# Finer scatter gates and earlier edge rows in the output stage of a graph network kernel

## What is computed

```python
h = jnp.maximum(_layernorm(x, axis=-1), 0.0)
...
h = _bn(jax.nn.relu(_gcn_conv(xn, src, dst, edge_weight, W1, b1, n)), g1, be1)
h = _bn(jax.nn.relu(_graph_conv(h, src, dst, edge_weight, Wrel2, brel2, Wroot2, n)), g2, be2)
h = _bn(jax.nn.relu(_graph_conv(h, src, dst, edge_weight, Wrel3, brel3, Wroot3, n)), g3, be3)
...
x = x + h
```

## Time and profile before

| | us |
|---|---|
| median of 3 runs | 3491.68 |
| the profiled execution, its own time | 3478.71 |
| its span, first to last instruction | 3476.9 |
| busy: TensorE, VectorE, ScalarE, GpSimd | 2853.6, 2650.0, 2361.0, 1376.2 |
| setup ends and `norm` starts at about | 38 |
| `norm` ends and `l1` starts at about | 483.6 |
| `out` starts at about | 2982 |

### The profile page before, as it was taken

One profiled execution on the slowest core, in us unless ns is written; L12 is line 12 of the kernel. 1 busy time (PEld: TensorE's weight loads), 2 busy tenths in 40 slices (PEclk: granted clock), 3 DMA queues, 4 the chain that ended last, 5 costly groups with the idle time before them and its releaser, 6 DMA issues. The chain is left out here.

```text
span 3476.9 us, 52252 instructions
## 1 busy us (share of the span) xinstructions
PE 2853.6 (82%) x12499; PEld 2035.4 (59%) x12641; DVE 2650.0 (76%) x5699; ACT 2361.0 (68%) x4168; POOL 1376.2 (40%) x1196
## 2 busy tenths in 40 slices
PE   3466549999999789999999999979999999544543
PEld 2455535555555467777777777656666666433432
DVE  6566638889898878888888888878999999533332
ACT  4577737777777578888888888667887887333331
POOL 1534556556666232111211111044433431266576
PEclk9788769999999899999999999999999999655555
DMA  5677638999999679999999999779999999799997
GB/s 195 219 244 267 228 129 315 356 329 360 343 360 355 254 283 350 351 358 352 364 355 356 355 355 357 254 269 329 353 355 358 358 351 334 285 366 361 381 357 231
DMA packets 335139, 1106.82 MB, mean 318 GB/s; under 512 B 54569, under 2 KB 102210, under 8 KB 285906
## 3 DMA queue, kind: packets, MB, share of 16 engines
q1 hardware_dynamic: 213412, 909.25, 71.3%
q0 software_dynamic: 62656, 77.70, 9.5%
q10 hardware_dynamic: 58990, 118.98, 9.4%
HBM read 599.13 MB, written 498.21 MB: 316 GB/s over the span
## 5 line engine op out<-in xcount | busy, mean ns | idle before, releaser
L1294 POOL DMA_INDIRECT l_ed_gathered<-agg_rows,pos_cols x392 | 457.4, 1167 | 1301.3 <-PE l_ps L1306 675.3
L1173 DVE TENSOR_TENSOR dense_tiles<-dense_tiles,l_dn_top 128x512 fp32r<-128x512 f32 x784 | 494.0, 683 | 140.6 <-ACT l_dn_top L1141 137.6
L1114 PE MATMUL l_ps<-l_dn_top,wroot_top 128*128 128x512 f32 x1176 | 485.6, 413 | 33.4 <-DVE dense_tiles L1173 14.0
L1114 PE MATMUL l_ps<-l_dn_top,wroot_rest 128*128 128x512 f32 x1176 | 467.6, 398 | 0.0
L1114 PE MATMUL l_ps<-dense_tiles,wroot_top 128*128 128x512 f32 x1176 | 466.8, 397 | 0.0
L1141 ACT ACTIVATE l_dn_top<-dense_tiles 128x512 fp32r<-128x512 f32 x784 | 447.7, 623 | 21.6 <-PEq L93 21.5
L640 PE MATMUL norm_ln_ps<-norm_ln_ho 128*128 128x130 f32 x1568 | 248.0, 321 | 183.1 <-ACT norm_ln_ho L628 100.3
L754 PE MATMUL l_ps<-l_dn_columns,w_fold 128*128 128x512 f32 x784 | 384.1, 612 | 9.9 <-ACT l_dn_ho L791 7.4
L628 ACT ACTIVATE norm_ln_ho<-norm_ln_x,norm_ln_nbias,norm_ln_rstd 128x128 f32<-128x128 f32 x784 | 304.0, 480 | 109.0 <-DVE norm_ln_nbias L581 105.9
L1763 PE MATMUL out_ps<-ident,dense_tiles 128*128 128x128 f32 x784 | 186.5, 417 | 205.7 <-ACT dense_tiles L1750 202.0
L1128 ACT ACTIVATE l_dn_ho<-l_ps,bias_fold 128x512 f32<-128x512 f32 x392 | 267.2, 685 | 128.5 <-PE l_ps L1114 124.5
(11 more groups left out here) (256 smaller groups left out, 6311.3 us busy)
## 6 DMA issues: line engine op xcount, KB each, us to landing
h_dense<-l_dn_ho SPq DMA_DIRECT2D x188, 1024.0 KB
dense_tiles<-h_dense SPq DMA_DIRECT2D x188, 1024.0 KB, 8.5
l_dn_rows<-h_rows SPq DMA_DIRECT2D x98, 520.0 KB
h_rows<-norm_ln_ho SPq DMA_DIRECT2D x97, 520.0 KB
h_dst<-l_ed_ho SPq DMA_DIRECT2D x98, 512.0 KB, 10.4
norm_ln_x<-in_x SPq DMA_DIRECT2D x97, 512.0 KB
x_tiles<-in_x SPq DMA_DIRECT2D x97, 512.0 KB, 6.4
out<-out_od_ot SPq DMA_DIRECT2D x97, 512.0 KB
```

Source lines behind the costliest of these rows:

```text
L1114: ins = pe.matmul(o, a, b, start=t == 0, stop=t == len(terms) - 1)
L1173: dve.tensor_tensor(rest[:, j, k, cc], hi[:, j, k, cc], top[:, j % 2, k, cc].bitcast(FP), ALU.subtract).then_inc(spl[j], 1)
L1294: pool.indirect_dma_start(tg[:, j, g, :], None, tab[n - 1][:, :], bass.IndirectOffsetOnAxis(ap=pos_c[:, t:t + 1], axis=0)).then_inc(gat[j] ...
```

## The change

Three things are changed.

First, in `out` the dense stages get a `head` of 4 slots, one round: the rows of edge chunks are made four tiles ahead. In the rounds of the order above the dense tiles stand one round later than before, and the edge chunks' scratch buffer lies in the memory of the statistics, which is free by then.

Second, in `norm` and in `out` the gate stands ahead of every chunk, and its unit is a **pair** of tiles (2048 nodes). The table has a row for each pair of slots.

Third, setup makes the table by integer shifts: last node, shifted right by 11, is the pair; shares of 2 or 4 slot pairs come by adding and shifting again.

```diff
+PAIR = 2 * W
-                sp.dma_start(last_node[:, 0:EI - 1], dst[0:(EI - 1) * ES * CW].rearrange("(o g e) -> o g e", o=1, g=EI - 1)[:, :, ES * CW - 1],
+                sp.dma_start(last_node[:, 0:EC - 1], dst[0:(EC - 1) * CW].rearrange("(o g e) -> o g e", o=1, g=EC - 1)[:, :, CW - 1],
...
-                for n in range(1, DI):
-                    dve.tensor_scalar(above[:, :, n - 1], last_f[:, :], float(n * NS * W), None, ALU.is_ge).then_inc(compared, 1)
-                dve.wait_ge(compared, DI - 1)
-                link(dve.tensor_reduce(count[:, 0, :], above[:, :, :], AXIS.X, ALU.add))
...
+                link(dve.tensor_scalar(last_pair[:, :], last_node[:, :], PAIR.bit_length() - 1, None, ALU.logical_shift_right))
+                for n in range(2):
+                    dve.tensor_scalar(shares_first[:, n, :], last_pair[:, :], 1, 2 - n, ALU.mult, ALU.add).then_inc(compared, 1)
...
-            firsts = [pool.value_load(table[0:1, row, g:g + 1], min_val=0, max_val=most) for row, (most, _) in enumerate(parts)]
-            for first, (_, slots) in zip(firsts, parts):
+            counts = [pool.value_load(table[0:1, row, g:g + 1], min_val=1, max_val=most) for row, (most, _) in enumerate(parts)]
+            for count, (_, slots) in zip(counts, parts):
                 for s in slots:
-                    pool.wait_ge(s, first * per + per)
+                    pool.wait_ge(s, count * per)
...
-                        if t % (ES * EG) == 0:
-                            gated(pool, rounds_norm, t // (ES * EG), 16, ((LI - 1, stored[0:2]), (LI - 2, stored[2:4]), (LI - 2, stored[4:8])))
+                        if t % EG == 0:
+                            gated(pool, tiles_norm, t // EG, 16, ((LI, stored[0:2]), (LI - 1, stored[2:4]), (LI - 1, stored[4:6]), (LI - 1, stored[6:8])))
...
+            head = slots if dense else 0
...
-                return slots, [(0, load)] + ([(slots - 1, store)] if dense else []), end if dense else None
+                return slots, [(head, load)] + ([(head + slots - 1, store)] if dense else []), end if dense else None
...
                     for k in range(EC):
                         pool.wait_ge(sm[k % slots], k // slots + 1)
-                        if k % ES == 0:
-                            gated(pool, rounds_first, k // ES, 16, ((DI - 1, dense_stored[0:2]), (DI - 2, dense_stored[2:4])))
+                        gated(pool, tiles_first, k, 16, ((DI, dense_stored[0:2]), (DI - 1, dense_stored[2:4])))
...
-                return slots, [(0, affine)], None
+                return slots, [(head, affine)], None
```

More of the change, by code:

```diff
@@ L279, in build @@
         ew_c = sb("weight_cols", [P, ET])
-        rounds_first = sb("rounds_first", [1, 2, EI], I32)
+        tiles_first = sb("tiles_first", [1, 2, EC], I32)
         zeros_c = sb("zeros_c", [128, 1])
@@ L303, in build @@
         moments = front_sb("moments0", [C, TC])
-        rounds_norm = front_sb("rounds_norm", [1, 3, EI], I32)
+        tiles_norm = front_sb("tiles_norm", [1, 4, EC], I32)
         mval = front_sb("map_values", [P, ET, 2])
@@ L331, in build @@
             pad_b, pad_m = ph.sb("pad_zero", [1, EP - E], U8), ph.sb("pad_mask", [1, EP - E], BF)
-            last_node, last_f = ph.sb("last_node", [1, EI], I32), ph.sb("last_node_f", [1, EI])
-            above, count = ph.sb("above", [1, EI, DI - 1]), ph.sb("rounds", [1, 5, EI])
+            last_node, last_pair = ph.sb("last_node", [1, EC], I32), ph.sb("last_pair", [1, EC], I32)
+            shares_first, shares_norm = ph.sb("shares_first", [1, 2, EC], I32), ph.sb("shares_norm", [1, 4, EC], I32)
             ones, zero_row = ph.sb("ones", [P, 128]), ph.sb("zero_row", [P, 2 * TC])
@@ L363, in _ @@
                 rows_of(sp, rows_f[:, 2, :, :], ew, rows_in)
-                sp.dma_start(last_node[:, 0:EI - 1], dst[0:(EI - 1) * ES * CW].rearrange("(o g e) -> o g e", o=1, g=EI - 1)[:, :, ES * CW - 1],
+                sp.dma_start(last_node[:, 0:EC - 1], dst[0:(EC - 1) * CW].rearrange("(o g e) -> o g e", o=1, g=EC - 1)[:, :, CW - 1],
                              allow_slow_non_contiguous=True).then_inc(last_in, 16)
-                sp.dma_start(last_node[:, EI - 1:EI], dst[E - 1:E].rearrange("(o t) -> o t", o=1)).then_inc(last_in, 16)
+                sp.dma_start(last_node[:, EC - 1:EC], dst[E - 1:E].rearrange("(o t) -> o t", o=1)).then_inc(last_in, 16)
                 sp.wait_ge(ds, STEPS)
@@ L489, in _ @@
                 dve.wait_ge(last_in, 32)
-                link(dve.tensor_copy(last_f[:, :], last_node[:, :]))
-                for n in range(1, DI):
-                    dve.tensor_scalar(above[:, :, n - 1], last_f[:, :], float(n * NS * W), None, ALU.is_ge).then_inc(compared, 1)
-                dve.wait_ge(compared, DI - 1)
-                link(dve.tensor_reduce(count[:, 0, :], above[:, :, :], AXIS.X, ALU.add))
[L495 to L500, removed]
+                link(dve.tensor_scalar(last_pair[:, :], last_node[:, :], PAIR.bit_length() - 1, None, ALU.logical_shift_right))
+                for n in range(2):
+                    dve.tensor_scalar(shares_first[:, n, :], last_pair[:, :], 1, 2 - n, ALU.mult, ALU.add).then_inc(compared, 1)
+                for n in range(4):
+                    dve.tensor_scalar(shares_norm[:, n, :], last_pair[:, :], 1, 4 - n, ALU.mult, ALU.add).then_inc(compared, 1)
+                dve.wait_ge(compared, 6)
+                dve.tensor_scalar(shares_first[:, :, :], shares_first[:, :, :], 1, None, ALU.logical_shift_right).then_inc(compared, 1)
+                dve.tensor_scalar(shares_norm[:, :, :], shares_norm[:, :, :], 2, None, ALU.logical_shift_right).then_inc(compared, 1)
+                dve.wait_ge(compared, 8)
+                dve.tensor_scalar(tiles_first[:, :, :], shares_first[:, :, :], 1, None, ALU.max).then_inc(compared, 1)
+                dve.tensor_scalar(tiles_norm[:, :, :], shares_norm[:, :, :], 1, None, ALU.max).then_inc(compared, 1)
+                dve.wait_ge(compared, 10)
                 for n, t in enumerate((src_c[:, :], dst_c[:, :], ew_c[:, :], out_c[:, :], mval[:, :, 1])):
@@ L1696, in output @@
             sto, gate = dense_stored, ph.sem(f"{name}_gate")
-            hi = ho_keep[:, :, 0, :] if dense else ph.sb(f"{name}_hi", [C, slots, groups * P])
+            hi = ho_keep[:, :, 0, :] if dense else stats.rearrange("c b g s -> c (b g s)")[:, 0:slots * groups * P].rearrange("c (j w) -> c j w", j=slots)
             xt = x_first
             held_over = lambda i: dense and isinstance(i, int) and i == 0
+            head = slots if dense else 0
             ot = ph.sb(f"{name}_ot", [P, slots, groups, C]) if dense else None
@@ L1764, in turn @@
                         ins.then_inc(tr[j], 1)
-                return slots, [(0, turn)], None
+                return slots, [(head, turn)], None
             def vector(dve):
@@ L1782, in add @@
                         ins.then_inc(sm[j], 1)
-                return slots, [(0, add)], None
+                return slots, [(head, add)], None
             return dict(sync=sync, gpsimd=gpsimd, scalar=scalar, tensor=tensor, vector=vector)
```

## The result

The changed kernel takes 3444.11 us, the median of 4 runs (3435.88 to 3447.02), beside 3492.09 for the one before: a ratio of 0.9858, 95% interval 0.9837 to 0.9878. That is 48 us faster, where +2.6 was forecast and 3484 was the lower end of the range. In the profiled executions the spans are 3439.8 and 3476.9, 37.1 apart.

The account below looks back on a forecast made before the run. The prediction took out to be bound by the dense tile stream, then GpSimd's scatters: tile 91's store landing + 42.9 us. Head +4.6, norm gates −2.0 and zeros gave +2.6 us, so 3494.3 us, range 3484 to 3503.

Parts of the forecast that it names:

- Gates at the end of `norm`: End of norm: chunks 46 to 48 released by their own gates, GpSimd ends at 472.54 instead of 474.54, gain 2.0 us.
- More table reads: cost 0: Gates, 49 instead of 25: the reads hide beneath the descriptor writing of the scatter ahead, cost 0.
- the idle of over 1 us: Chunk borders in out: forecast to show 0.30 idle; over 1 us there would show the prediction wrong.
- The rival's own sum: Slower rival, uncovered reads at borders 45 to 48: 4 × 1.3 = 5.4, total +8.0 us, 3499.7; chance 0.14.
- The tail of `out`: End of out: chunk 44 still waits for tile 91's store, then 20 scatters with one pause take 42.9 us; gain 0.
- Once in 60: Scatters of out: GpSimd waits about 6 us for its queued scatters to drain, at the 61st, 121st and 181st.
- The head: Start of out: chunk 1's load (3.80) and work (0.81) come ahead of tile 0, which starts 4.6 us later.
- the rival to which I gave 0.05: Start of out: chunk 1 lands sooner, in 2.58 us; head costs 3.4, total +1.4, 3493.1; chance 0.05.
- Chunk 3 has a wait for its load too: Start of out: a second wait of ScalarE, at chunk 3, was named as a sign that the prediction is wrong.
- The 3.80 of the earlier trace: Start of out: time from issue of chunk 1's load to ScalarE's start in the kernel before, taken for the head.
- The estimate of 2.6 us: Start of out: chunk 1's 256 KB load from about 2.0 us fixed cost plus bytes over 436 GB/s; head would cost 3.4.
- Setup: Setup's table: eleven small operations replace 30, hidden beneath VectorE's wait for an unrelated load; change 0.

Follow-up runs that it names:

- e3: The changed kernel, with norm's first scatter held back until the first 40 tiles are stored; ratio 1.0048 to the kernel before, norm 455.5 us.
- e6: The kernel before, all old limits kept, with norm's gate repeated, already open, ahead of the odd chunk; ratio 0.9948 to the kernel before, norm 424.7 us.
- e9: The kernel before, with each scatter of norm writing 16 of its 128 rows; one run, only norm is read: 456.7 us.
- e4: The kernel before, with GpSimd in norm waiting after every fourth scatter until all have landed; ratio 0.9996 to the kernel before, norm 440.9 us.

## Why the prediction was wrong

**The step that failed** is "Gates at the end of `norm`", −2.0 us, which measured −47. I took the dense part of `norm` as given and worked out only how GpSimd's last three chunks stand to the last stores. That the end of `norm` is GpSimd's was right: 9.1 us lie between GpSimd's last scatter and `l1` in both kernels (473.63 + 0.91 to 483.64, 426.06 + 0.91 to 436.07). But the stores to which it stands come 51 us earlier (the last one's issue at 413, not 464), because VectorE is held up less by the scatters (its waits are 50 us shorter). And the end itself isn't as I drew it: GpSimd finishes 14 us after that issue, not the 8.4 of my sum.

What I didn't look at was there: VectorE's waits in `norm`, 130 us, with "remote" beside steps that wait for VectorE alone; and a DMA share of 0.42 beside 24 scatters, in a phase where I counted GpSimd as a follower. I had no rival in which scatters slow the engine that feeds their own gates.

**"More table reads: cost 0"** was read from one border of `out`, with two reads and scatters of 1.86 us. It holds in the last 20 scatters, where chunks 46 to 48 open at 0.30. Further ahead it doesn't: the new gates of odd chunks show 1.4 to 1.7 us again and again (1.71 at 3371.30), where the kernel before shows 0.30; that is the idle of over 1 us that the prediction named as a sign of being wrong. It costs nothing because GpSimd waits 11.44 us for a store afterwards, not because the reads are covered. (The rival's own sum is also off a little: 4 × 1.3 is 5.2, not 5.4.) For `norm`, with four reads and scatters of 1.27, I priced nothing. The reads aren't always covered there (e3, e6), and their pauses are a gain, not a cost.

**The tail of `out`** was right: chunk 44 starts after a longer idle time (11.44), released by a store, and 20 scatters with one pause of 6.77 at the 181st take 3433.15 − 3389.88 = 43.3 us, against 42.9. "Once in 60" isn't the whole of these pauses, though: the kernel before has one more, 5.78 us, ahead of the 114th scatter of `out`.

**The head** was right as a sum, +4.6 forecast, 4.7 in the profile, but by luck, for its parts were wrong. Chunk 1's load took 2942.80 − 2940.31 = 2.49 us, not 3.80, so tile 0 starts 3.2 late; that is the rival to which I gave 0.05. The rest came further on, at least in part where a tile of the first loads waits 4.47, beside 2.97 for the same tile before; why isn't traced. Chunk 3 has a wait for its load too (2.48), which the prediction had named as a sign of being wrong; before, chunk 1 waited 2.87 in that place, so it adds nothing. The 3.80 of the earlier trace rows was a load among others; here it went alone. The estimate of 2.6 us from the Trainium skill ("DMA: Bandwidth & Descriptors", "Anatomy of one DMA — SWDGE (gpsimd) path") is close to the 2.49, though the page fits it to DMAs that GpSimd issues, and SyncE issued this one.

**Setup** is 0.5 shorter, as good as nothing. (The small operations that went are 32, not 30.)

## What to carry to other kernels

Where a stage's end is set by a follower, ask first why what it follows isn't faster: a stretch in which no engine but the follower is busy is the place to look. Read waits of an engine on itself; they should be short (in the kernel before no more than 0.17 us at the first five scatters of a run), and when they aren't, look at what other engines do at that moment. A cost that is paid as a pause can be a gain for someone else, so price an added wait on every engine beside it, not only on its own.

## What the runs showed of the hardware

- With indirect DMAs issued by GpSimd in a row (every 1.27 us), VectorE's wait for its own semaphore signals grows, to 0.4 to 2.6 us in the run shown. In the kernel before, whose pauses are all over 2.5 us, this begins at the sixth (at the first five none of some 670 instructions waits over 0.17); in the changed kernel, with short pauses, it also comes earlier. It doesn't go with the bytes of a scatter (e9) nor with a full DMA stream (share 0.42).
- In the records, the signals of other engines go the same way. In the kernel before, the trace shows the semaphore's update within 0.15 us of the end of 32 of 35 TensorE instructions between runs, of 8 of 29 at the first to fifth scatter, and of none of 26 from the sixth on; for ScalarE these are 20 of 25, 17 of 39 and 5 of 25. A missing one can be late or not recorded. The scatters' own semaphore, raised 16 times by each of 196 scatters, has 553 recorded updates before, 954 in the changed kernel and 2234 in e4: the fewer, the longer VectorE waits. That points at the path of the signals, or at their recording, and not at VectorE. No run tells the instruction, its packets and its completion signals apart, and every execution on record was profiled, so a share of the recording itself isn't excluded.
- A pause of 3.3 to 5.3 us after every four of them frees VectorE (e4: 22 us of waits of the normalisation instead of 130). Pauses mostly of 1 to 3 us free it in part (80).
- The Trainium skill ("SBUF — State Buffer", "SBUF: two separate sides") tells of a lock between VectorE and GpSimd that one holds for a whole instruction while the other blocks. These rows look different: in the kernel before the first five scatters of a run delay nothing, VectorE's instructions keep their length, and what is late is the signal behind them.
